# Mixture-of-experts weights in longer rows: three DMA issues an expert in place of four

## The reference, cut to what matters

```python
E, K, H, I = 64, 6, 512, 352         # experts, picks a token, features, inner width
scores = softmax(x @ gate_w.T); topk_w, topk_i = top_k(scores, K)
buf[e, slot] = x[token]              # up to 64 tokens an expert
g = einsum('ech,ehi->eci', buf, w_gate)
u = einsum('ech,ehi->eci', buf, w_up)
y = einsum('eci,eih->ech', silu(g) * u, w_down)
out = weighted sum of each token's picks + silu(x @ sw_gate) * (x @ sw_up) @ sw_down
```

## Time and profile before

| what | us |
|---|---|
| median of the 3 runs shown | 3053.68 |
| lowest and highest of them | 3049.96, 3054.82 |
| span of the profiled execution, first to last instruction | 3057.4 |
| first expert stage, first to last pair's start | 1119.2 to 1546.1 |
| second expert stage, the same (its last 29 pairs) | 2625.6 to 3032.2 |

### The profile page before, as it was taken

One profiled execution on the slowest core, in us unless ns is written; L12 is line 12 of the kernel. 1 busy time (PEld: TensorE's weight loads), 2 busy tenths in 40 slices (PEclk: granted clock), 3 DMA queues, 4 the chain that ended last, 5 costly groups with the idle time before them and its releaser, 6 DMA issues.

```text
span 3057.4 us, 37567 instructions
## 1 busy us (share of the span) xinstructions
PE 2742.0 (90%) x13484; PEld 1445.2 (47%) x13484; DVE 1789.4 (59%) x3787; ACT 1298.1 (42%) x2689; POOL 1529.0 (50%) x944
## 2 busy tenths in 40 slices
PE   4668889898998879988868999999899999999998
PEld 2455555555555534333325555555544444444443
DVE  5899999999999742222236666665624444222222
ACT  4557576675866411110107666766722220111111
POOL 6999999999999702212125555555500001121211
PEclk7769999998998989989979999999999999999999
DMA  5344544545545479999960000000225323999997
GB/s 194 141 167 153 195 172 161 192 155 182 180 167 174 141 273 352 340 336 341 336 201 1 29 29 29 29 29 15 89 87 181 121 86 130 312 334 336 342 348 219
DMA packets 198955, 557.76 MB, mean 182 GB/s; under 512 B 24880, under 2 KB 26800, under 8 KB 198256
## 3 DMA queue, kind: packets, MB, share of 16 engines
q1 hardware_dynamic: 180624, 513.27, 48.7%
q0 software_dynamic: 17088, 40.90, 5.8%
q10 hardware_dynamic: 1056, 1.18, 0.1%
HBM read 479.50 MB, written 75.79 MB: 182 GB/s over the span
## 4 chain that ended last, share of the span: by engine, by line
PE 54%; DVE 3%; ACT 2%; POOL 2%; issue 2%; DMA 1%; POOLq 0%; SPq 0%; DVEq 0%; ACTq 0%
PE bank L1133 11%; PE bank L1159 5%; PE bank L1036 5%; PE bank L1057 5%; PE bank L1071 5%; PE bank L1184 5%; PE bank L1241 4%; PE bank L1218 3%; PE bank L1206 2%; PE bank L1230 2%; POOL arena L1940 2%; PE bank L1116 1%; PE bank L1172 1%; ACT arena L1763 1%; PE bank L1043 1%
## 5 line engine op out<-in xcount | busy, mean ns | idle before, releaser
L1844 POOL TENSOR_TENSOR arena<-arena 128x1024 f32<-128x1024 f32 x256 | 607.5, 2373 | 7.9 <-PE bank L986 5.0
L1692 ACT ACTIVATE bank<-arena 128x512 f32<-128x512 f32 x512 | 346.6, 689 | 317.6 <-DVE arena L1330 198.5
L986 PE MATMUL bank<-arena 128*128 128x128 f32 x2048 | 306.3, 303 | 146.1 <-POOL arena L1850 145.8
L1940 POOL TENSOR_TENSOR arena<-arena 128x2048 f32<-128x2048 f32 (+3 forms) x128 | 296.9, 2323 | 276.4 <-DVE arena L1560 276.3
L986 PEld LDWEIGHTS bank<-arena 128*128 128x128 f32 x2048 | 260.4, 156 | 231.7 <-POOL arena L1850 186.2
L1763 ACT ACTIVATE arena<-arena 128x256 f32<-128x256 f32 (+3 forms) x512 | 287.3, 566 | 148.8 <-DVE arena L1551 125.2
L1133 PE MATMUL bank<-arena 128*64 128x352 f32 x2048 | 343.1, 491 | 0.0
L1850 POOL TENSOR_TENSOR arena<-arena 128x512 f32<-128x512 f32 x256 | 333.8, 1304 | 17.5 <-DVE arena L1330 17.5
L1330 DVE TENSOR_TENSOR_SCAN arena<-bank,arena 128x512 f32<-128x512 f32 x256 | 310.7, 1214 | 26.5 <-POOL arena L1844 19.4
L1330 DVE TENSOR_TENSOR_SCAN bank<-bank,arena 128x512 f32<-128x512 f32 x256 | 308.4, 1205 | 0.0
L1057 PE MATMUL bank<-arena 128*128 128x512 f32 x640 | 288.3, 593 | 7.6 <-ACT arena L1719 7.6
(11 more groups left out here) (145 smaller groups left out, 4159.0 us busy)
## 6 DMA issues: line engine op xcount, KB each, us to landing
arena<-scratch_bc SPq DMA_DIRECT2D x128, 1024.0 KB, 5.4
arena<-in_w_gate SPq DMA_DIRECT2D x128, 704.0 KB
arena<-in_w_up SPq DMA_DIRECT2D x128, 704.0 KB
arena<-in_w_down SPq DMA_DIRECT2D x128, 512.0 KB
arena<-in_w_down SPq DMA_DIRECT2D x128, 192.0 KB
scratch_x<-arena SPq DMA_DIRECT2D x16, 1024.0 KB, 4.5
scratch_xn<-arena SPq DMA_DIRECT2D x15, 1024.0 KB, 4.1
arena<-scratch_x SPq DMA_DIRECT2D x44, 256.0 KB, 6.0
```

Source lines behind the costliest of these rows:

```text
L986: i = nc.tensor.matmul(y[:, t * P:(t + 1) * P], w[:, n, t * P:(t + 1) * P], p.ident, is_transpose=True, start=False, stop=g == GROUPS - 1 ...
L1692: nc.scalar.activation(bank[p.da_bank(k, n)][:, :], block_of(p.dt, b, c), ACT.Exp, scale=p.alog[:, c, state:state + 1]).then_inc(*p.decaye ...
L1844: nc.gpsimd.tensor_tensor(out=p.hb[k % HB], in0=over(block_of(p.dtx, b, c), 1, NG), in1=p.bc[k // 2 % NBC][:, 0], op=ALU.mult).then_inc(*p ...
L1940: nc.gpsimd.tensor_tensor(out=own, in0=own, in1=over(p.rden[:, k % 2, :], 2, width), op=ALU.mult).then_inc(*p.divided.up(k))
```

## The change

The host lays the weights out anew. w_in holds, for each expert and partition, the gate's and then the up's four chunks: one row of 11264 B, which goes to 128 partitions in one DMA. w_out holds each partition's rows of down behind each other: partitions 0 to 95 have three (6144 B) and go in one DMA of 96 partitions, partitions 96 to 127 have two (4096 B) and go in another of 32 partitions. The bytes moved are the same. Buffers stay where they were, and so do the waits, apart from up's semaphore, which now counts one DMA an expert. What TensorE reads is the same memory.

```diff
     def weight_memory(self, sb, m, n):
-            ring.append((sb.cut([HC, INTER]), sb.cut([HC, INTER]), sb.cut([IC, H])))
+            ring.append(self.weight_views(sb.cut([2, HC * INTER]), sb.cut([IC, H])))
+
+    def weight_views(self, both, down):
+
+        up = [both[:, w, :].rearrange("p (c i) -> p c i", c=HC) for w in range(2)]
+        return (*up, down, both.rearrange("p w i -> p (w i)"), down.rearrange("p j h -> p (j h)"))
...
-        self.up_in = [sig(f"up_in{r}", "w_up", parts=range(2), by=16,
-                          where=lambda m, e, i, r=r: e % RING_W[m] == r) for r in range(max(RING_W))]
+        self.up_in = [sig(f"up_in{r}", "w_up", by=16, where=lambda m, e, r=r: e % RING_W[m] == r)
+                      for r in range(max(RING_W))]
...
-            PE.wait_ge(p.up_in[e % nw], m, e, 1)
+            PE.wait_ge(p.up_in[e % nw], m, e)
...
-        for w, name in ((0, "w_gate"), (1, "w_up")):
-            nc.sync.dma_start(f["ring"][r][w], d[name][e].rearrange("(p c) i -> p c i", c=HC)).then_inc(
-                *p.up_in[r].up(m, e, w))
+        nc.sync.dma_start(f["ring"][r][3], d["w_in"][e]).then_inc(*p.up_in[r].up(m, e))
...
-        nc.sync.dma_start(dn[:, 0:2, :], d["w_down"][e, 0:2 * P, :].rearrange("(j p) h -> p j h", p=P)).then_inc(
-            *p.down_in[r].up(m, e, 0))
-        nc.sync.dma_start(dn[0:LAST_I, 2, :], d["w_down"][e, 2 * P:, :]).then_inc(*p.down_in[r].up(m, e, 1))
+        dn = f["ring"][r][4]
+        nc.sync.dma_start(dn[0:LAST_I, :], d["w_out"][e, :LAST_I * IC * H].rearrange(
+            "(p n) -> p n", p=LAST_I)).then_inc(*p.down_in[r].up(m, e, 0))
+        nc.sync.dma_start(dn[LAST_I:P, 0:(IC - 1) * H], d["w_out"][e, LAST_I * IC * H:].rearrange(
+            "(p n) -> p n", p=P - LAST_I)).then_inc(*p.down_in[r].up(m, e, 1))
```

More of the change, by code:

```diff
@@ L695, in last_weights @@
         sb.at = routing
-        self.ff[0]["ring"].append((sb.cut([HC, INTER]), sb.cut([HC, INTER]), down))
+        self.ff[0]["ring"].append(self.weight_views(sb.cut([2, HC * INTER]), down))
         assert sb.at <= after
@@ L2090, in w_down @@
         r = e % nw
-        dn = f["ring"][r][2]
         if e >= nw:
             SP.wait_ge(p.rings[1 + 2 * m].made, "down", m, (e - nw) // 2)
-        nc.sync.dma_start(dn[:, 0:2, :], d["w_down"][e, 0:2 * P, :].rearrange("(j p) h -> p j h", p=P)).then_inc(
-            *p.down_in[r].up(m, e, 0))
-        nc.sync.dma_start(dn[0:LAST_I, 2, :], d["w_down"][e, 2 * P:, :]).then_inc(*p.down_in[r].up(m, e, 1))
+        dn = f["ring"][r][4]
[3 more added lines that the diff above has]
+            "(p n) -> p n", p=P - LAST_I)).then_inc(*p.down_in[r].up(m, e, 1))
     def route1(m, q):
@@ L2187, in lay_out @@
     c = np.ascontiguousarray
+    down = np.pad(g["L0_ffn_w_down"], ((0, 0), (0, IC * P - INTER), (0, 0)))
+    full = down.reshape(E, IC, P, H).transpose(0, 2, 1, 3)
     return {
@@ L2197, in lay_out @@
         "gate_wT": c(g["L0_ffn_gate_w"].T),
-        "w_gate": c(g["L0_ffn_w_gate"]), "w_up": c(g["L0_ffn_w_up"]), "w_down": c(g["L0_ffn_w_down"]),
+        "w_in": c(np.concatenate([g[n].reshape(E, P, HC * INTER) for n in ("L0_ffn_w_gate", "L0_ffn_w_up")], axis=2)),
+        "w_out": c(np.concatenate([full.reshape(E, P, IC * H)[:, :LAST_I].reshape(E, -1),
+                                   full.reshape(E, P, IC * H)[:, LAST_I:, :(IC - 1) * H].reshape(E, -1)], axis=1)),
         "sw_gate": c(g["L0_ffn_sw_gate"]), "sw_up": c(g["L0_ffn_sw_up"]), "sw_down": c(g["L0_ffn_sw_down"]),
```

## The result

| kernel | median of the runs, us | lowest to highest |
|---|---|---|
| before | 3053.62 | 3049.96 to 3054.82 |
| changed | 3179.87 | 3149.56 to 3235.99 |

The changed kernel takes 1.0347 times as long (95% interval 1.0317 to 1.0377), about 106 us more; the medians of all five runs are 126 us apart. The forecast was 3206 us, slower. The changed kernel's times scatter by 2.7%, those of before by 0.2%. The ratio leaves out its two longest runs, and as the profiled execution (span 3221.7 us) is one of them, I read a later execution of the same kernel, 3187.7 us, and name it "changed".

A forecast was written before the change was run, and what follows sets the result against it. DMA was taken to bound the first expert stage, TensorE the second with DMA also full. Per pair 6.9 + 7.6 + 2.4 = 16.9 us, 2.6 over 14.3; times 58.5 pairs, 152 us more: 3206 us, range 3046 to 3330.

The forecast's parts named there:

- The dips: Weight fetches: the DMA rate falls once an expert, to 228 to 282 GB/s early on; read as transfers over part of the partitions.
- Gate and up, 420 against 412 GB/s: Expert stages: one DMA of 11264 B rows takes 6.9 us a pair, down from 7.0, a gain of 0.1 us.
- The term for down: Expert stages: all of down in partial transfers at 189 GB/s, 7.6 us a pair against 4.9, a loss of 2.7 us.
- before's budget: First expert stage: 14.3 us of DMA a pair, 2.4 indirect queue, 9.8 whole transfers, 2.1 left for 96 partitions.
- The 208 GB/s that I named as one end: Down's partial transfers: 189 raised by 412/375; with 160 as the other end, the forecast's cases lie from 3167 to 3288 us.
- equal growth, 76 us each: Both expert stages were to grow by about 76 us each, while the rest keeps its time.
- Signs that I named: Stages: stretches near 420 stay, dips well below 300; second stage: TensorE gaps, SyncE's 158.4 us of waits shrink, clock leaves 1.00.
- The clock: TensorE, second stage: falls from 1.00; at 0.92 its 14.3 us become 15.5, still below 16.9, so no cost.
- The faster one: Rival, expert stages: only row length counts, down above about 295 GB/s, 46 us gained, 3008 us; chance 0.13.
- The price for each transfer: Rival, expert stages: each partial transfer costs 0.5 us whatever its bytes, 14.8 us a pair, 3083 us; chance 0.14.
- Longer packets that hold up the scatter: Rival, first stage: scatter rows wait behind 11264 B rows, 1.7 us a pair, 54 us, 3108 us; chance 0.05.
- Half of the groups at their full rate: Rival, down: 64 or 32 partitions share eight groups at 210 GB/s, a pair stays 14.3 us, 3054 us; chance 0.05.

The follow-up runs named there:

- The padded kernel: Changed kernel with down padded by zeros to three rows on every partition, one DMA of 128 partitions by 6144 B: 3012.84 us, ratio 0.986.
- the halves: Same zero-filled rows and bytes as the 3012.84 us kernel, but down goes in two DMAs, partitions 0 to 63 and 64 to 127: 3256.62 us, ratio 1.0654.
- the bare loads: Programs with only weight loads, no computing, 8 experts at once or 48 through a ring of 6; a pair takes 13.1 us changed, 11.9 before.
- the padded kernel with short rows: Kernel before, with down padded to 384 rows and fetched by one DMA of 128 partitions by three 2048 B rows: 3015.93 us, ratio 0.9866.
- up-alone: Kernel before, with only gate and up changed to one DMA of 11264 B rows, down as before: 3053.16 us, ratio 0.999.

## Why the prediction was right, and where it was not

**Direction and mechanism: right.** The dips were read as the mark of transfers over part of the partitions, not of short rows. The padded kernel, the halves and the bare loads each show it by themselves. The other half of the mechanism, that a partial transfer holds up the long rows behind it, is not borne out by the bare loads, where the mix runs as its parts do. Only the slices of the kernel's first stage look like it.

**What bounds each stage: right.** The first stage was bound by DMA, and gained when DMA got quicker. TensorE bound the second, which could only lose.

**Gate and up, 420 against 412 GB/s: right by themselves.** The bare load has 427, and the run with this half alone shows no change. Beside long partial rows they do not keep that rate: the stretches near 420, which were to stay, are gone from the first stage's slices.

**The term for down: too dear by itself.** I took 189 GB/s for partial transfers, from the rest of before's budget. For before the total is confirmed, 11.9 us for the mix alone; how it divides is not, since the 2.1 us left for 96 partitions hang on my 375 GB/s for whole rows of 2048 B, which the padded kernel with short rows suggests was low. But long partial rows do better: 13.1 less 6.8 for gate and up at 427 leaves 6.3 us for 1.44 MB, 229 GB/s. So the sum should have been 15.6 us a pair, 1.3 above before, not 2.6. The 208 GB/s that I named as one end was the nearer.

**That the sum came so near was in part luck.** Two errors went against each other. The forecast charged 2.6 us to each of 58.5 pairs, 152 us. In the trace 37 pairs lose (24 in the first stage, 13 in the second), and they lose 3.5 us each in the first and 2.3 in the second, 114 us in all; another 9 us come before the first stage and 7 behind the second, both of which I had put at nothing. What I missed is the stock: weights that were fetched ahead cover slower loads for the first 18 intervals of the second stage. So equal growth, 76 us each, failed: 84 and 30. While the stock lasts the loads of the second stage take 15.9 us a pair (67.92 MB of q1 from 2750 to 3000), near the 15.6 of the bare mix; the first stage takes 17.5. Some of that excess goes with the depth of SyncE's backlog; the rest, and the scatter from run to run, stays open. No run put the kernel's own gathers and scatters, or computing, beside the bare loads.

**Signs that I named.** In the first stage the dips below 300 came. In the second TensorE got gaps ahead of line 1132, but small ones, 8.4 us in the whole stage and 11.2 more ahead of line 1164, and SyncE's waits for the up product did not shrink: 185.1 us from 2700 to 3000 where they were 158.4.

**The clock: half right.** It fell in the first stage, 0.92 to 0.86, and in the second only in the part that lost time, to 0.97 from 2937 us on. There TensorE needs 197.2 us for the 897 matmuls that took 188.6, so of the 29.6 us lost 8.6 are longer work and the rest is idle time. I had put the clock at nothing; whether those 8.6 us would have been idle at full clock, no run shows. In the padded kernel it rose to 0.98, and the first stage ran at 12.1 us a pair (374.9 us over 31 intervals), below the 12.5 that I had as TensorE's floor.

**The rivals.** The faster one would have needed 295 GB/s for down; it was 229, and the up-alone and short-row runs show that row length moves nothing here that the total shows. The price for each transfer is refuted by the halves. Longer packets that hold up the scatter are refuted by the up-alone run, which has the 11264 B rows beside the kernel's own scatters and loses nothing. Half of the groups at their full rate was right for the loads by themselves where I had given it 0.05: it had 210 GB/s for 64 and for 32 partitions, and the bare loads have 206 and 202. It fails at 96, where its two terms make 315 and 254 was measured, and at the time, 3054 us.

## What to carry to other kernels

Look at how many partitions a transfer reaches before its row length. Fetching zeros to fill 128 partitions (3% more bytes) beat the exact fetch by 1.3%, where loads of 96 partitions run at 60% of the full rate. A busy share of 1.03 on the DMA engines says nothing of what they deliver: read the GB/s beside it, in slices short enough to see each transfer. And before you multiply a loss by the number of pairs, ask how many of them live on weights fetched ahead: here 18 intervals of the second stage lost nothing.

## What the runs showed of the hardware

- Rate of a load by partitions reached, 6144 B rows, engines fully busy: 128: 420, 96: 254, 64: 206 GB/s; 32 with 4096 B rows: 202 to 215, the higher from the first to the last packet's time. So 96 partitions carry 1.23 times what 64 do, not 1.5 times, and 32 are as good as 64.
- Two halves, lower and upper, issued one behind the other: 229 GB/s, not 420.
- Kernels with down in 96 and 32 partitions scatter most: 0.9 to 2.7% from the lowest to the highest time in six sets of runs, against 0.2% in the two kernels with whole transfers only (3011.24 to 3016.24 us with long rows). Partial transfers alone do not make it, since the kernel with halves scatters by 0.4%.
- A wait that keeps SyncE from queueing far ahead can make a kernel faster: here by 31 us, with gate and up landing 17.8 us after their issue in place of 46.2. How it does so is not shown.
- Weights fetched ahead can hide slower loads for long: the second stage kept its pace for 18 intervals (263.8 us against 263.3) before it lost 2.3 us a pair.
